# Mask products of the masked experts moved into the first attention, kept as bf16; six buffers for the sorted chunks; shared raw weight buffers

## Chip, cores and metric

The kernel runs on one core of one Trainium2 chip. The metric is the device time of one execution in microseconds. Its engines are TensorE (PE), VectorE (DVE), ScalarE (ACT), GpSimd (POOL) and SyncE (SP, which here issues nearly all transfers). Each works through its own instructions in order and waits for the others by semaphores. SBUF has 128 partitions; PSUM has eight banks of 128x512 f32.

## The reference, cut to what matters

A decoder of two layers over x of 4 x 256 tokens of width 256; after every part comes x = layernorm(x + part(x)). The change touches the first three parts.

```python
# 1: causal attention, 16 heads of 128, weights w_q, w_k, w_v, w_o
x = _layernorm(x + _L0_attn_ref(x, ...))
# 2: a graph: sim = mean over heads of Q K^T of ctx_512
threshold = top_k(sim, 76)[..., -1:]
A = sigmoid(sim) * (sim >= threshold)
A = (A + swapaxes(A)) * 0.5
x = _layernorm(x + (1 - gamma) * x + gamma * A)
# 3: 32 masked experts that share one weight
top1_w, top1_idx = max(softmax(x @ router_w.T))
w_q = clip(round(weight / 0.5), -1, 1)
for e in range(32):
    y = x @ (w_q * scale[:, None] * expert_masks[e]).T
    out = where(top1_idx == e, y * top1_w, out)
x = _layernorm(x + out)
# 4: attention with rotary positions, 5: cross attention, 6: 16 routed experts
```

## The kernel before

The program is a row of blocks: setup, attention layer 0, graph_and_masked_experts, attention layer 1, and the rest. In a block every engine has its own instruction list, and a new block starts on all engines once the old one is finished on all of them.

**First attention.** 16 steps s, each with two heads of two batches; two steps use one group g of weights. In step s PE makes the scores of step s+1, the projections of step s+2, the transposed probabilities and their products with the values; in odd steps also the next group's values and the output projection. POOL splits each raw f32 weight into a high and a low part (split_proj, split_v, split_o, lines 392 and 395), running up to two steps ahead of PE. SP loads the raw weights of group g as soon as the split of the group before has freed their one buffer: q and k after split_proj, v after split_v, o after split_o. Besides, DVE searches each row's 76th largest sim in eight rounds spread over the steps (its copy is L975), and near the end (keep, L993 and L996) sets the entries below it to zero, using the raw q and k buffers for the tanh values. POOL also splits kv and kvt for later use (split_keys) and makes the ternary weight c.tern at s = 9.

**Masked experts.** The 32 masks, each 256x256 f32 (256 KB), are handled in 16 pairs. SP loads a pair into one of four raw buffers (two of their own, c.kv and c.kvt). POOL multiplies pairs 0 to 11 with c.tern (L1345), DVE pairs 12 to 15 (L1518), into four bf16 buffers. PE transposes a pair into one of two PSUM banks (turn, L1381) and ACT copies it to the weight array w (copied, L1458), bank by bank. Meanwhile DVE and POOL do norm 1 (moments L1079 and L1082, roots L1103 to L1110, applied in L1505 together with the graph's entries), norm 2 (applied in L1511), then x is transposed and split (L1143, L1149, L1155), the router's logits are made (L1185, L1186, L1193), DVE finds each row's expert (L1535 to L1543), PE counts ranks (L1388, L1391) and DVE works out each row's place among the sorted rows (L1551 to L1566). POOL scatters the rows to DRAM by eight indirect transfers (L1356). Then come six chunks of 512 sorted rows: a chunk is loaded (L1311) into one of two buffers, turned by PE (L1401), split by ACT and DVE (L1465, L1585), and multiplied with each tile's expert weight (L1417, L1418). ACT evicts to one of two staging buffers (L1474), SP stores them (L1318), and POOL gathers all rows back (L1362). A chunk's buffer is loaded again when the chunk has been turned; SP issues these loads between the stores. keep_warm (L134) issues products on an idle tile.

The last part of SP's list in before:

```python
weights.first_loads(sp)
sp.wait_ge(s_scattered, 16 * NT)
...
sorted_load(0)
sorted_load(1)
for q in range(CHUNKS):
    if q + 2 < CHUNKS:
        sorted_load(q + 2)
    for r in range(2 * q, 2 * q + 2):
        store(r)
```

Of the kernel before, what the change touches and what calls it, by code (L numbers as in the profile page):

```python
# [67 lines left out]
def decoder(nc, a, out):  # L68
    with ExitStack() as ctx:
# [23 lines left out]
        c.ffn_weight, c.clipped, c.tern = sb("ffn_weight", [P, KC, D]), sb("clipped", [P, KC, D]), sb("tern", [P, KC, D], BF16)  # L93
# [242 lines left out]
class AttentionWeights:  # L336
# [12 lines left out]
    def __enter__(self):  # L349
# [4 lines left out]
        self.raw = {n: sb(f"raw_{n}", shape[n]) for n in "qkvo"}  # L354
# [24 lines left out]
    def first_loads(self, sp):  # L379
        for n in "kqvo":  # L380
            self.load(sp, n, 0)
# [36 lines left out]
    def second_splits(self, pool):  # L418
        self.split_all(pool, "v", 0, self.s_split_v)

# [34 lines left out]
def attention(c, layer, weights):  # L455
# [36 lines left out]
    with ExitStack() as ctx:  # L492
# [48 lines left out]
        with nc.Block() as block:  # L541
            @block.sync
            def _(sp):
                for g in range(1, LAST_GROUP + 1):
# [13 lines left out]
            def _(pool):  # L558
# [24 lines left out]
                def ternary():  # L583
# [6 lines left out]
                    nc.gpsimd.tensor_scalar(c.tern[:], c.ffn_weight[:], -12582912.0, None, ALU.add)  # L590

# [5 lines left out]
                def split_keys(part):  # L597
# [15 lines left out]
                    elif part == 3:  # L613
# [3 lines left out]
                        nc.gpsimd.tensor_tensor(c.kvg_lo[:], weighted, f32(c.kvg_hi[:]), ALU.subtract)  # L617
# [11 lines left out]
                for s in range(LAST + 1):  # L629
# [10 lines left out]
                    if not rope and s == 9:  # L640
                        ternary()

# [420 lines left out]
class Norm:  # L1063
# [34 lines left out]
    def root(self, pool, half, eps=EPS, factor=None, squares=None):  # L1098
# [3 lines left out]
        if squares is None:  # L1102
            self.nc.gpsimd.tensor_scalar(self.shifted[:, part], self.mv[:, part, 1], eps, None, ALU.add)  # L1103
# [9 lines left out]
    def roots(self, pool, factor=None):  # L1113
# [52 lines left out]
class Router:  # L1166
# [3 lines left out]
    def __init__(self, c, name, sb, w, experts, raw_banks, out):  # L1170
        self.c, self.nc, self.w, self.experts, self.raw_banks, self.out = c, c.nc, w, experts, raw_banks, out
        self.flat = sb(f"{name}_flat", [2 * experts, NTOK])
# [36 lines left out]
def graph_and_masked_experts(c, weights):  # L1209
# [22 lines left out]
    DVE_PAIRS = range(12, PAIRS)  # L1232
    YBANKS, YSTEPS = 4, -(-TILES0 // 2)
    MAGIC = 12582912.0
    with ExitStack() as ctx:
# [6 lines left out]
        router = Router(c, "b_router", sb, c.rt, EXPERTS0, (c.banks[4], c.banks[6]), c.banks[5])  # L1242
# [725 lines left out]
```

## Time and profile before

| what | value |
|---|---|
| median of 3 runs | 927.09 us (926.79 to 928.6) |
| profiled execution, its own time | 930.73 us |
| its span, first to last instruction | 928.9 us |
| PE busy | 811.1 us (87%) |
| DVE busy | 594.8 us (64%) |
| POOL busy | 492.2 us (53%) |
| ACT busy | 429.9 us (46%) |
| mean granted TensorE clock | 0.943 of full speed |

The profiled execution took 1.8 us more than its span. Busy shares are means over stages with different limits. The first attention runs to about 327.5 us, the masked experts from 327.8 to about 455 us, and the second attention follows.

### The profile page before, as it was taken

The numbers are of one execution on the slowest core, as the hardware profiler recorded it, in microseconds if no ns is written. First come the engines' busy times: TensorE is split into PE (matmuls) and PEld (weight loads), VectorE is DVE, ScalarE is ACT, GpSimd is POOL, SyncE is SP. The second block draws the span as 40 slices with busy tenths as digits, with TensorE's granted clock in tenths as the row PEclk, the third lists the DMA queues.
The fourth block names the chain that finished last, engine by engine and source line by source line (L and its number), as shares of the span: only waits on it lengthen the run. The fifth ranks groups of instructions, "written<-read, shape, count | busy, mean of one in ns | idle before, by whom it ended". The sixth has DMA issues, their size and how long they took to land. (4 is left out here: it accounts for less than half of the span.)

```text
span 928.9 us, 14587 instructions
## 1 busy us (share of the span) xinstructions
PE 811.1 (87%) x4745; PEld 691.0 (74%) x4745; DVE 594.8 (64%) x1655; ACT 429.9 (46%) x1209; POOL 492.2 (53%) x407
## 2 busy tenths in 40 slices
PE   7899999999999836583788999999888499999995
PEld 5678888888888725282477888888776288888885
DVE  4796876866966599311666777767655745455555
ACT  5264644634635515152356665566563532322223
POOL 4757368647440166703255546464521447777774
PEclk8999999999999958897799999999999789999998
DMA  6220620220200057453001110111001001111111
GB/s 194 69 91 1 227 91 1 91 92 1 91 23 1 1 165 238 163 158 91 29 0 53 52 51 3 51 52 52 16 8 36 11 18 51 51 51 34 50 40 46
DMA packets 58331, 59.09 MB, mean 64 GB/s; under 512 B 5392, under 2 KB 49312, under 8 KB 58272
## 3 DMA queue, kind: packets, MB, share of 16 engines
q1 hardware_dynamic: 57504, 56.24, 19.5%
q0 software_dynamic: 768, 2.10, 0.7%
q8 instruction: 32, 0.52, 0.2%
q14 instruction: 27, 0.22, 0.1%
HBM read 50.00 MB, written 8.32 MB: 63 GB/s over the span
## 5 line engine op out<-in xcount | busy, mean ns | idle before, releaser
L829 ACT ACTIVATE a_probs<-bank,a_neg_peak 128x128 f32<-128x128 f32 (+1 forms) x256 | 103.5, 429 | 91.8 <-DVE a_neg_peak L937 91.8
L857 ACT ACTIVATE a_probs<-a_probs,a_row_inv 128x128 f32<-128x128 f32 (+1 forms) x256 | 92.0, 447 | 19.8 <-DVE a_row_inv L945 19.8
L937 DVE CUSTOM_DVE_ANT_0 bank<-bank,causal 128x128 f32<-128x128 f32 (+1 forms) x256 | 82.5, 393 | 20.3 <-PE bank L699 19.2
L835 ACT ACTIVATE a_probs_t<-bank 128x512 f32<-128x512 f32 x96 | 53.9, 597 | 75.7 <-PE bank L719 75.7
L1694 POOL TENSOR_TENSOR d_h_lo<-d_h,d_h_hi 128x512 fp32r<-128x512 f32 x40 | 51.8, 1297 | 52.8 <-ACT d_h_hi L1813 39.3
L738 PE MATMUL bank<-a_probs_t,a_vals 128*128 128x256 f32 x256 | 76.5, 380 | 0.0
L392 POOL TENSOR_TENSOR a_wk_hi<-a_raw_k,one 128x512 fp32r<-128x512 f32 (+1 forms) x24 | 21.7, 902 | 102.4 <-DMA a_raw_k<-in_L_attn_w_k_dram 39.7
L112 PE MATMUL bank<-a_wo_hi,a_ot_hi 128*128 128x256 f32 x256 | 74.4, 291 | 0.7 <-DVE a_ot_lo L957 0.7
L1899 DVE TENSOR_TENSOR d_h<-d_silu,bank 128x512 f32<-128x512 f32 x40 | 27.5, 688 | 73.2 <-PE bank L114 73.1
L113 PE MATMUL bank<-a_wo_lo,a_ot_hi 128*128 128x256 f32 x256 | 73.0, 285 | 0.0
L114 PE MATMUL bank<-a_wo_hi,a_ot_lo 128*128 128x256 f32 x256 | 73.0, 285 | 0.0
L134 PE MATMUL bank<-idle 128*128 128x512 bf16 x110 | 36.6, 505 | 34.1 <-DVE x L1591 15.2
L1906 DVE SCALAR_TENSOR_TENSOR x<-bank,d_gate,x 128x256 f32<-128x256 f32 x160 | 64.6, 476 | 2.6 <-PE bank L114 0.2
L113 PE MATMUL bank<-xt_lo,d_w_hi 128*128 128x512 f32 x160 | 64.0, 400 | 0.0
L112 PE MATMUL bank<-xt_hi,d_w_hi 128*128 128x512 f32 x160 | 63.9, 399 | 0.0
L114 PE MATMUL bank<-xt_hi,d_w_lo 128*128 128x512 f32 x160 | 63.8, 399 | 0.0
L705 PE MATMUL bank<-a_keys,a_queries 128*128 128x256 f32 x256 | 62.3, 388 | 0.0
L719 PE MATMUL bank<-ident,a_probs 128*128 128x128 f32 x384 | 53.4, 275 | 6.1 <-ACT a_probs_t L835 6.1
L719 PEld LDWEIGHTS bank<-ident,a_probs 128*128 128x128 f32 x384 | 44.3, 140 | 16.5 <-ACT a_probs_t L835 10.8
L581 POOL TENSOR_TENSOR a_queries<-sim 128x512 f32<-128x512 f32 x32 | 40.7, 1278 | 29.2 <-DVE sim L912 29.2
L912 DVE TENSOR_TENSOR sim<-bank,a_sin 64x512 f32<-64x512 f32 x80 | 55.1, 688 | 1.1
L829 ACT ACTIVATION_READ_ACCUMULATOR a_probs<-bank,a_neg_peak 128x1 f32 x256 | 55.1, 215 | 0.0
(303 smaller groups left out, 2454.3 us busy)
## 6 DMA issues: line engine op xcount, KB each, us to landing
d_raw<-in_L_ffn_we_dram SPq DMA_DIRECT2D x48, 128.0 KB, 2.2
a_raw_k<-in_L_attn_w_k_dram SPq DMA_DIRECT2D x8, 512.0 KB, 6.3
a_raw_q<-in_L_attn_w_q_dram SPq DMA_DIRECT2D x8, 512.0 KB, 5.3
a_raw_v<-in_L_attn_w_v_dram SPq DMA_DIRECT2D x8, 512.0 KB, 7.2
a_raw_o<-in_L_attn_w_o_dram SPq DMA_DIRECT2D x8, 512.0 KB, 3.7
b_raw<-_L_ffn_expert_masks_dram SPq DMA_DIRECT2D x16, 256.0 KB, 3.2
a_raw_q<-in_L_attn_Wq_dram SPq DMA_DIRECT2D x8, 512.0 KB, 4.9
a_raw_o<-in_L_attn_Wo_dram SPq DMA_DIRECT2D x8, 512.0 KB, 3.6
```

The costliest lines, as they stand in the source:

```text
L112: nc.tensor.matmul(out, l_hi, r_hi, start=start, stop=False)
L113: nc.tensor.matmul(out, l_hi, r_lo, start=False, stop=False)
L114: return nc.tensor.matmul(out, l_lo, r_hi, start=False, stop=stop)
L705: last = nc.tensor.matmul(out, queries[:, j, row + P:row + T], keys[:, j % keys.shape[1], row:row + width], start=True, stop=True)
L719: last = nc.tensor.transpose(c.banks[3 + turned % 2][:, slot % 4 * P:(slot % 4 + 1) * P], probs[s % 2][:, i, at:at + P], c.ident[:])
L738: nc.tensor.matmul(out, vals_of(s)[:, 2 * i, cols], probs_t[:, at:at + T], start=True, stop=False)
L829: nc.scalar.activation(probs[s % 2][:, i, at:at + width], c.banks[i][:, at:at + width], ACT.Exp, bias=neg_peak[:, n:n + 1], scale=-1.0, ac ...
L835: nc.scalar.activation(probs_t[:, i * BANK:(i + 1) * BANK], c.banks[3 + (3 * s + i) % 2][:], ACT.Copy).then_inc(s_pt_free, 1)
L857: last = nc.scalar.activation(part, part, ACT.Copy, scale=row_inv[:, s % 2, n + r:n + r + 1])
L912: last = nc.vector.tensor_tensor(two(across[to:to + HALF_BLOCK, n % 2]), two(bank[at:at + HALF_BLOCK]), many(sin[at:at + HALF_BLOCK], HALF ...
L937: last = nc.vector.tensor_tensor_reduce(part, part, mask, -1.0, 3e38, ALU.add, ALU.min, neg_peak[:, n + r:n + r + 1])
L1906: last = nc.vector.scalar_tensor_tensor(c.x[:, t], c.banks[4 + u][:, (t % 2) * D:(t % 2 + 1) * D], g, c.x[:, t], ALU.mult, ALU.add, accum_ ...
```

## The change

- A new object Masks makes all 16 masked pairs on POOL during the first attention and keeps them all, as bf16: eight pairs in a new tile c.spare, two where the ternary weight was made (c.small), and two each in the raw v, o and q weight buffers. The raw masks pass through c.kv and c.kvt. SP issues their loads within the attention's list, and POOL makes pairs 0, 1 in step 10, 2, 3 in step 12, 4, 5 in step 13, 6 to 11 in step 14 and 12 to 15 in the last step, once DVE has kept its entries.
- The raw weight buffers belong to the program now and are shared by both attentions.
- In the masked experts DVE and POOL make no masks. PE turns eleven pairs before x is transposed, in place of three pairs and twelve warming products, and the others between the router's steps. DVE's small operations on the counters stand ahead of the subtractions of the transposed x.
- The factor of norm 1's root, 2 - gamma, is put into the power's argument as its square's reciprocal, made once in the first attention.
- Six chunk buffers: all six loads are issued one after the other once the scatters have landed, with one semaphore for chunk 0, one for 1 and 2, one for 3 to 5.
- The next attention's raw o weights are loaded behind the last store, and its v weights are split once the last chunk has been turned. Several small tiles move into c.sim.

```diff
+        c.less_sq, c.minus_two = sb("less_sq", [P, 1]), sb("minus_two", [P, 1])
+        c.raw = {n: sb(f"raw_{n}", [DH, GROUP, D] if n == "o" else [P, KC, GROUP * DH]) for n in "qkvo"}
+        c.spare = sb("spare", [P, 4, 2 * BANK])
+        c.masks = Masks(c)
...
+class Masks:
+    PAIRS, RAW = EXPERTS0 // 2, 2
+
+    def __init__(self, c):
+        self.c, self.nc = c, c.nc
+        as_pair = lambda ap: ap.rearrange("p (e k d) -> p e k d", e=2, k=KC)
+        flat = lambda ap: ap.rearrange("p k n -> p (k n)")
+        self.raw = [as_pair(flat(c.kv[:])), as_pair(c.kvt[:])]
+        homes = [flat(home).bitcast(BF16) for home in (c.spare[:], c.small[:], c.raw["v"][:], c.raw["o"][:], c.raw["q"][:])]
+        size = 2 * KC * D
+        self.masked = [as_pair(home[:, at:at + size]) for home in homes for at in range(0, home.shape[-1], size)]
+        self.AFTER_VALUES, self.AFTER_KEPT = 10, 12
...
+    def load(self, sp, pair):
+        if pair == 0:
+            sp.wait_ge(self.s_spare, 1)
+        elif pair >= self.RAW:
+            sp.wait_ge(self.s_masked, pair - self.RAW + 1)
+        for e in range(2):
+            sp.dma_start(self.raw[pair % self.RAW][:, e], self.c.a["L0_ffn_expert_masks"][2 * pair + e].rearrange("(k p) i -> p k i", p=P)).then_inc(self.s_raw[pair % self.RAW], 16)
+
+    def mask(self, pool, pair):
+        pool.wait_ge(self.s_raw[pair % self.RAW], (pair // self.RAW + 1) * 32)
+        wide = self.c.tern[:].unsqueeze(1).broadcast_to([P, 2, KC, D])
+        self.nc.gpsimd.tensor_tensor(self.masked[pair], self.raw[pair % self.RAW], wide, ALU.mult).then_inc(self.s_masked, 1)
...
@@ attention, SP @@
                         sp.wait_ge(s_split_v, g)
                         weights.load(sp, "v", g)
+                    if not rope and g == LAST_GROUP:
+                        for pair in range(4, 6):
+                            c.masks.load(sp, pair)
                     sp.wait_ge(s_split_o, g)
                     weights.load(sp, "o", g)
+                    if not rope and g >= 5:
+                        for pair in ((0, 1), (2, 3), range(6, c.masks.PAIRS))[g - 5]:
+                            c.masks.load(sp, pair)
...
@@ attention, GpSimd @@
+                MASKED_AT = {10: (0, 1), 12: (2, 3), 13: (4, 5), 14: range(6, c.masks.AFTER_KEPT), LAST: range(c.masks.AFTER_KEPT, c.masks.PAIRS)}
+
+                def masks(s):
+                    for pair in MASKED_AT.get(s, ()):
+                        if pair == c.masks.AFTER_KEPT:
+                            pool.wait_ge(s_kept, 1)
+                            pool.drain()
+                        c.masks.mask(pool, pair)
...
@@ Norm.root @@
-            self.nc.gpsimd.tensor_scalar(self.shifted[:, part], self.mv[:, part, 1], eps, None, ALU.add)
+            self.nc.gpsimd.tensor_scalar(self.shifted[:, part], self.mv[:, part, 1], eps, factor, ALU.add, ALU.mult)
...
-        if factor is not None:
-            pool.drain()
-            last = self.nc.gpsimd.tensor_scalar(self.rstd[:, part], self.rstd[:, part], factor[:], None, ALU.mult)
...
@@ masked experts, SP @@
-                for pair in range(RAW):
-                    load(pair)
                 sp.dma_start(numbers[:], a["numbers"]).then_inc(s_numbers, 16)
-                for pair in range(RAW, PAIRS):
-                    load(pair)
-                weights.first_loads(sp)
+                sp.wait_ge(s_turned, PAIRS)
+                weights.first_loads(sp, "kqv")
                 sp.wait_ge(s_scattered, 16 * NT)
-                sp.wait_ge(s_masked, DVE_PAIRS.start)
-                sp.wait_ge(s_masked_dve, len(DVE_PAIRS))
-                sorted_load(0)
-                sorted_load(1)
                 for q in range(CHUNKS):
-                    if q + 2 < CHUNKS:
-                        sorted_load(q + 2)
+                    sp.dma_start(sorted_x[q], c.sorted_rows[slots_of(q)].rearrange("(t p) d -> p t d", p=P)).then_inc(s_sorted[load_of[q]], 16)
+                for q in range(CHUNKS):
                     for r in range(2 * q, 2 * q + 2):
                         store(r)
+                sp.wait_ge(s_stored[1], 16 * CHUNKS)
+                weights.load(sp, "o", 0)
...
@@ masked experts, GpSimd @@
-                norm1.roots(pool, c.one_less)
-                for pair in range(0, 2):
-                    mask(pair)
+                norm1.roots(pool, c.less_sq[:])
                 norm2.roots(pool)
-                for pair in range(2, DVE_PAIRS.start):
-                    mask(pair)
...
+                pool.wait_ge(s_turned, PAIRS)
                 weights.first_splits(pool)
+                pool.wait_ge(s_xt, XT + CHUNKS * KC)
                 weights.second_splits(pool)
...
@@ masked experts, TensorE; ScalarE's copies go in the same order @@
-                    pe.wait_ge(s_sorted[q % 2], 16 * (q // 2 + 1))
+                    pe.wait_ge(s_sorted[load_of[q]], 16 * len(LOADED[load_of[q]]))
...
-                for pair in range(0, 3):
+                for pair in range(0, 11):
                     turn(pair)
-                norm1.wait(pe, 1)
-                keep_warm(c, 12)
                 turned2.pe(pe, s_norm2, 4)
-                for pair in range(3, 5):
+                for pair in range(11, 13):
                     turn(pair)
                 router.raw_pe(pe, turned2)
-                for pair in range(5, 7):
-                    turn(pair)
+                turn(13)
                 router.logits_pe(pe)
-                for pair in range(7, 9):
+                for pair in range(14, PAIRS):
                     turn(pair)
                 rank()
-                for pair in range(9, PAIRS):
-                    turn(pair)
...
@@ masked experts, VectorE @@
-                turned2.dve(dve)
...
                 nc.vector.tensor_scalar(numbers[:], numbers[:], -float(EXPERTS0), None, ALU.add)
+                turned2.dve(dve)
...
-                for pair in DVE_PAIRS:
-                    mask(pair)
```

## Rows read from the trace of the kernel before

**Rows 1.** The page, its first line.

```profile
span 928.9 us, 14587 instructions
```

**Rows 2.** Windows: length; busy PE, PEld, DVE, ACT, POOL (count); PE clock, DMA share, GB/s.

```profile
94.00:130.00 36.00, 36.00 (x212) 31.67 (x211) 26.98 (x87) 18.18 (x58) 20.80 (x14) 1.00 0.42 143
...
328.00:374.00 46.00, 23.16 (x191) 17.41 (x192) 42.72 (x80) 18.79 (x23) 32.23 (x22) 0.70 0.71 223
```

**Rows 3.** Timeline of DVE, 331 to 374 us: start, duration, engine, line, operation.

```profile
331.72 1.67 DVE L1505 SCALAR_TENSOR_TENSOR x<-x,b_b_norm_rstd,sim 128x256 f32<-128x256 f32 x4 [0.28 <-POOL b_b_norm_rstd L1110]
...
335.24 3.76 DVE L1505 SCALAR_TENSOR_TENSOR x<-x,b_b_norm_rstd,sim 128x256 f32<-128x256 f32 x4
...
340.86 10.90 DVE L1511 SCALAR_TENSOR_TENSOR x<-x,b_b_norm_mv,b_b_norm_rstd 128x256 f32<-128x256 f32 x8
...
353.13 1.29 DVE L1155 TENSOR_TENSOR xt_lo<-bank,xt_hi 128x512 fp32r<-128x512 f32 x2 [0.18 <-ACT xt_hi L1149]
...
360.19 0.41 DVE L1535 TENSOR_REDUCE b_top<-bank 128x8 f32<-128x256 f32 x1
...
361.20 1.33 DVE L1539 SCALAR_TENSOR_TENSOR b_found<-b_above,b_numbers 128x256 f32<-128x256 f32 x1
...
363.10 1.69 DVE L1543 TENSOR_TENSOR b_chosen<-b_found,b_first 128x256 bf16<-128x256 f32 x1
...
369.47 1.22 DVE L1518 TENSOR_TENSOR ffn_weight<-kvt,tern 128x1024 bf16<-128x1024 f32 x1
370.61 0.18 DVE L1551 TENSOR_SCALAR b_segments<-bank 128x32 f32<-128x32 f32 x1
...
373.45 0.17 DVE L1566 CAST b_place<-b_place_f 128x8 uint32<-128x8 f32 x1
```

**Rows 4.** Timeline of POOL, its first masks.

```profile
333.55 4.38 POOL L1345 TENSOR_TENSOR b_masked<-b_raw,tern 128x1024 bf16<-128x1024 f32 x2
```

**Rows 5.** Timeline of PE and ACT, 356 to 374 us.

```profile
356.54 1.97 PE L1193 MATMUL bank<-pick,b_b_router_flat 64*128 64x32 f32 x16
...
365.06 1.17 PE L1391 MATMUL bank<-b_chosen,b_every 128*128 128x256 bf16 x8
...
369.34 4.69 ACT L1458 ACTIVATE b_w<-bank 128x1024 fp32r<-128x1024 bf16 x5 [0.28 <-PE bank L1381]
```

**Rows 6.** The chunks: PE's timeline, PE's waits (total, times, longest), the loads' landing.

```profile
391.97 1.09 PE L1401 MATMUL bank<-ident,kvt 128*128 128x128 f32 x8 [0.25 <-DMA kvt<-sorted_rows]
...
PE bank L1401 <- DMA kvt<-sorted_rows: 3.4, 3, 2.0
...
DMA to landing us min/median/max: 3.8/4.5/5.3
```

**Rows 7.** POOL and DVE by time; SP's issue of a mask pair; L975 in all; mask loads' landing.

```profile
108.74 1.04 POOL L392 TENSOR_TENSOR a_wk_hi<-a_raw_k,one 128x512 fp32r<-128x512 f32 x1 [16.93 <-PE bank L114]
...
127.76 0.98 DVE L975 COPY a_work<-sim 128x256 f32<-128x256 f32 x1
...
242.25 1.04 POOL L392 TENSOR_TENSOR a_wk_hi<-a_raw_k,one 128x512 fp32r<-128x512 f32 x1 [7.52 <-DMA a_raw_k<-in_L_attn_w_k_dram]
...
301.74 1.89 POOL L392 TENSOR_TENSOR a_wo_hi<-a_raw_o,one 128x1024 fp32r<-128x1024 f32 x1 [31.32 <-PE bank L114]
...
314.92 1.67 DVE L996 SCALAR_TENSOR_TENSOR sim<-sim,thr,a_raw_k 128x256 f32<-128x256 f32 x4
...
326.24 1.28 DVE L964 TENSOR_TENSOR x<-x,bank 128x512 f32<-128x512 f32 x2
...
344.70 0.88 SPq L1305 DMA_DIRECT2D kv<-_L_ffn_expert_masks_dram  x2
...
L975 DVE COPY a_work<-sim x8: 281/283/4250, 35.3 to 270.7; 128x256 f32<-128x256 f32 x8
...
DMA to landing us min/median/max: 2.8/3.3/5.5
```

More of the change, by code:

```diff
@@ L92, in decoder @@
         c.rows = sb("rows", [P, 5, D])
-        c.ffn_weight, c.clipped, c.tern = sb("ffn_weight", [P, KC, D]), sb("clipped", [P, KC, D]), sb("tern", [P, KC, D], BF16)
+        c.small = sb("small", [P, 2, KC * D])
+        c.ffn_weight, c.clipped = (c.small[:, i].rearrange("p (k d) -> p k d", k=KC) for i in range(2))
+        c.tern = sb("tern", [P, KC, D], BF16)
         c.s_ffn_weight, c.s_rows = c.sem("ffn_weight"), c.sem("rows")
@@ L377, in load, with first_loads @@
         sp.dma_start(self.raw[n][:], part).then_inc(self.s_raw[n], 16)
-    def first_loads(self, sp):
-        for n in "kqvo":
+    def first_loads(self, sp, which="kqvo"):
+        for n in which:
             self.load(sp, n, 0)
@@ L616, in split_keys @@
                         pool.drain()
-                        nc.gpsimd.tensor_tensor(c.kvg_lo[:], weighted, f32(c.kvg_hi[:]), ALU.subtract)
+                        nc.gpsimd.tensor_tensor(c.kvg_lo[:], weighted, f32(c.kvg_hi[:]), ALU.subtract).then_inc(c.masks.s_spare, 1)
                 if rope:
@@ L641, in _ @@
                         ternary()
+                    if not rope:
+                        masks(s)
             @block.tensor
@@ L1096, in squares, with root @@
             last.then_inc(self.s_var, 1)
-    def root(self, pool, half, eps=EPS, factor=None, squares=None):
+    def root(self, pool, half, eps=EPS, factor=1.0, squares=None):
         part = slice(HALF_TILES[half].start, HALF_TILES[half].stop)
@@ L1241, in graph_and_masked_experts @@
         turned3 = Transposed(c, "b_turned", turned2, XT + CHUNKS * KC)
-        router = Router(c, "b_router", sb, c.rt, EXPERTS0, (c.banks[4], c.banks[6]), c.banks[5])
-        top, above, likely = sb("top", [P, NT]), sb("above", [P, NT, EXPERTS0]), sb("likely", [P, NT, EXPERTS0])
+        router = Router(c, "b_router", sb, c.rt, EXPERTS0, (c.banks[4], c.banks[6]), c.banks[5], flat=c.sim[0:2 * EXPERTS0, 0:NTOK // T].rearrange("p t n -> p (t n)"))
+        top = sb("top", [P, NT])
+        above, likely, found = (c.sim[:, NT // 2 + i].rearrange("p (t e) -> p t e", t=NT) for i in range(3))
         total, weight = sb("total", [P, NT]), sb("weight", [P, NT])
-        numbers, found, first = sb("numbers", [P, NT, EXPERTS0]), sb("found", [P, NT, EXPERTS0]), sb("first", [P, NT])
+        numbers, first = sb("numbers", [P, NT, EXPERTS0]), sb("first", [P, NT])
         chosen = sb("chosen", [P, NT + 1, EXPERTS0], BF16)
@@ L1297, in _ @@
             def _(sp):
-                def load(pair):
-                    if pair >= RAW:
-                        if pair - RAW in DVE_PAIRS:
-                            sp.wait_ge(s_masked_dve, pair - RAW - DVE_PAIRS.start + 1)
-                        else:
-                            sp.wait_ge(s_masked, pair - RAW + 1)
-                    for e in range(2):
-                        sp.dma_start(raw[pair % RAW][:, e], a["L0_ffn_expert_masks"][2 * pair + e].rearrange("(k p) i -> p k i", p=P)).then_inc(s_raw[pair % RAW], 16)
-                def sorted_load(q):
-                    if q >= 2:
-                        sp.wait_ge(s_xt, XT + KC * (q - 1))
-                    sp.dma_start(sorted_x[q % 2], c.sorted_rows[slots_of(q)].rearrange("(t p) d -> p t d", p=P)).then_inc(s_sorted[q % 2], 16)
                 def store(r):
@@ L1485, in _ @@
                 nc.scalar.activation(likely[:], above[:], ACT.Exp).then_inc(s_likely, 1)
-                for pair in range(9, PAIRS):
-                    copied(pair)
                 high(0)
```

60 lines of the change are left out of this document (24 added, 36 removed).

## The prediction

> **What bounds the kernel now.** I read the page first for the span [rows 1], then busy time by stage [rows 2], then the timelines of VectorE (DVE), GpSimd (POOL), TensorE (PE) and ScalarE (ACT) in the stages that the change touches. In a stretch of the first attention PE is busy for the whole of it: 36.00 of 36.00 us [rows 2]. PE sets the time there, and whatever DVE or POOL does is free until it makes PE wait. In the stretch from 328 to 374 us it is the other way round: PE is busy 23.16 of 46 us at a granted clock of 0.70, DVE 42.72 us [rows 2]. Here the chain runs through DVE: two normalizations, the router, the choice of expert, the place of each row.
>
> DVE is busy there but mostly not at work. The same operation on the same 128x256 tile takes 0.42 us each in one group of four and 0.94 us each in the next, and the eight that follow take 1.36 us each [rows 3]. The slow ones lie under POOL's mask products, 2.2 us each [rows 4]. Subtractions that read PSUM, further on, keep their 0.64 us [rows 3]. So operations whose inputs are all in SBUF wait for POOL's current instruction. Four masks made by DVE itself, 1.22 us each, then stand between the choice of expert and the places: DVE chose at 364.79 (363.10 + 1.69) and reads the ranks only at 370.61 [rows 3].
>
> **The stage with the normalizations.** I follow DVE with all masks gone from DVE and POOL.
> 1. The scale factor of the first norm goes into the power's argument, and the POOL operation L1110 falls away. DVE idled 0.28 us for it before L1505 [rows 3]: gain 0.3.
> 2. The second group of L1505 takes 1.67 instead of 3.76 us [rows 3]: gain 2.1.
> 3. L1511 runs eight times in 10.90 us; at 0.42 each it is 3.3 [rows 3]: gain 7.6. POOL's second-norm root comes about 1.6 us after its moments, while the other half's tile work takes 1.7, so it stays just hidden. Were it not, up to 1 us is lost. Sum 10.0.
> 4. Seven small DVE operations (the counters) now precede the four subtractions. Uncovered by POOL I take 1.2 us for them, from 0.28 for a 128x256 copy [rows 7] and 0.17 or 0.18 for the small ones [rows 3]; bounds 0.6 and the 5.8 us that they span now (354.4 to 360.2 [rows 3]). On the path: loss 1.2.
> 5. The last subtraction ends at 354.42 and the router's logits at 358.51 (356.54 + 1.97 [rows 5]), 4.1 us later, but DVE reads them at 360.19 since the small operations are still under way [rows 3]. With those moved ahead, the 4.1 us remain of 5.8: gain 1.7.
> 6. L1539 and L1543 take 1.33 and 1.69 us; at 0.42 each that is a gain of 2.2 [rows 3].
> 7. After the choice only the rank products remain: they end at 366.23 (365.06 + 1.17 [rows 5]). DVE starts at 370.61, and could at 366.3: gain 4.3.
>
> The places, ready at 373.62 [rows 3], so come 10.0 - 1.2 + 1.7 + 2.2 + 4.3 = 17.0 us earlier. The scatters and all behind them hang on the places and move with them.
>
> **What has to hide there.** Sixteen pairs still pass through PE and ACT. ACT copies five in 4.69 us, 0.94 each [rows 5]; eleven from 328.9 on (the block's start and one turn of about 1 us) end at 339.3, and the first normalized half is ready at 340.2 by my steps. Only 0.9 us of cover: if PE stays at the low clock, each of its turns is as long as a copy, and 1 us may show. The twelve warming products are gone as well; the bound for a low clock in transposes and router is 0 to 2 us. The pace of 0.94 us already had PE at high clock, so I take 0. The other five pairs lie between steps whose DVE work is longer.
>
> **The sorted chunks.** In before PE waited 3.4 us in three waits for the transfer of a chunk, 0.25 of it ahead of the second [rows 6]. With six buffers these go. But chunks 1 and 2 now share a semaphore: the second turn waits for the third transfer. Landing ran from 3.8 to 5.3 us, the second of two queued behind the first [rows 6], so a third queued is some 1.5 us later still. Net gain 3.4 - 0.25 - 1.5 = 1.6; bounds -1.5 (nothing won, since the stores' two buffers become the limit) and 3.1. The value weights' split waits for the last chunk's turn now and ends, 4.3 us of POOL work later, well ahead of the last store; the output weights' load goes behind the stores, where the next attention needs it only after its first two head pairs.
>
> **The first attention.** POOL takes sixteen masks instead of twelve: 35 us in all. It has the room: it idled 31.32 us before 301.74 alone [rows 7].
> - SP's queue: after each output weight load come mask loads, 1 MB before the next q, k and v. POOL's split behind them begins at 242.25 now, 7.5 us waited for its transfer [rows 7]. Two masks (4.4 us) push the output split and so the loads; four mask loads add 2 us of issue (0.88 for two [rows 7]) and up to 3 of transfer. I get 251 instead of 242.25. The same position four weight groups earlier was as late in before: its split began at 108.74 after a wait of 16.93 [rows 7], where the one at 242.25 had waited 7.5. PE had 36.00 of 36.00 in that stretch [rows 2]. So this lateness costs nothing. SP also stands at the load of pair 4 until mask 2 is done; behind it is only the output load, due at 301.74.
> - Pairs 6 to 11 alternate between two raw buffers: a load takes 0.9 to issue and 3.3 to land [rows 7], a mask 2.2 [rows 4], so two pairs need 6.5 us. From 280 on they end near 299, ahead of the last output split at 301.74 [rows 7].
> - DVE's copy L975 takes 0.28 us as a rule, took 0.98 under POOL at 127.76, within the full stretch, and once 4.25 [rows 7]. Two more may meet POOL work, up to 2.2 us each: I take 0.3, bounds 0 and 4.4.
>
> The Trainium skill, "SBUF — State Buffer", section "Who interferes with whom", says that a DVE copy in a two-port mode, or a DVE operation with both inputs in SBUF against a POOL operation that reads SBUF, is blocked for the other's whole instruction. By that rule alone, with both blocked copies charged to PE, the sum would be 4.4 us worse; the trace agrees with the blocking (0.98 for 0.28) and not with the charge.
>
> - The tail: pairs 12 to 15 wait until DVE has kept its entries, at 316.59 (314.92 + 1.67 [rows 7]). Masks 12 and 13 end at 321.1; load 14 is issued at 319.0 and lands at 323.2, load 15 at 321.1 and 325.4; mask 15 ends at 327.6. DVE's last addition ends at 327.52 [rows 7], and the next block starts for all engines together behind it. I charge 0.3. With landings of 5.5 us, the maximum [rows 7], it is 2.5; nothing is below 0.
>
> The skill, "GPSIMD Engine Reference", section 4.1, advises against GpSimd for a two-input elementwise operation, at about twice DVE's time. The trace agrees (2.2 against 1.22 us). Were the four pairs moved from DVE all exposed in the tail, it would take 4 us from the gain.
>
> **Sum.** 17.0 + 1.6 - 0.3 - 0.3 = 18.0 us. The profiled execution took 930.73 us around a span of 928.9 [rows 1], so 912.7; it is 3.6 above the median of the runs, 927.09, from which I subtract the same: 909.1 us.
>
> **Rivals.**
> - A, as above: 906.5 to 913, chance 0.62.
> - B, the stall is gone but PE and ACT hold the stage: low clock, the eleven copies as a gate (2 to 3 us), stores limiting the chunks (3), tail late (2.5). For it speaks the clock of 0.70 [rows 2]. 913 to 919, chance 0.25.
> - C, more gain than summed (small operations 0.6, chunks 3.1, second norm's wait none): 904 to 906.5, chance 0.07.
> - D, slower: the raw buffers' pace. If pairs 6 to 11 needed over 7 us each instead of 3.3, mask 11 would end past 313; the output split queues behind it on POOL, DVE's ten keeping operations wait 1 to 1.8 us each for the masks, and the last four masks end 18 us late, at 345.5, where all gain is spent. At 9 us each it would be about 935. Against it: landings of 3.3 and at most 5.5 us with an otherwise idle queue. Chance 0.03.
> - E, PE waits for a late projection split and gives back most: 919 to 927, 0.03, against which the 108.74 row stands.
>
> Measurement can tell 0.2%, 1.9 us, from no change. Faster: A, B, C and most of E, 0.95; same 0.02; slower 0.03. The range takes A with part of B and C: 905.5 to 916.5.
>
> **What would show it.** Right: L1505 and L1511 near 0.42 us each; places some 29 us after the block's first moments, which begin at 327.8, instead of 45.8; no wait of PE for a chunk after the second; the first attention's stretch still full. Wrong: PE idle for a POOL split between 200 and 300; a mask on POOL after DVE's last addition; PE at low clock from the first turn to the router; evictions waiting for stores in every chunk.

## The result and the profile after

The changed kernel takes 902.47 us (median of 4 runs, 900.31 to 906.13), the kernel before 926.94 on the same chip: a ratio of 0.974 with a 95% interval of 0.970 to 0.978. The gain is 24.5 us, against 18.0 forecast, and the time lies 3 us below the range's lower end. A second comparison in five rounds gave 901.38 us and 0.9743 (0.9717 to 0.9768). Times of different groups of runs below come from different chips, on which the kernel before had medians of 926.5 (both kernels again, late weights, idle delay), 926.54 (masks put back, chunk loads) and 924.37 us (everything with warming products); across groups the ratios to the kernel before are the fair comparison.

The span of the changed kernel's profile is 901.7 us, with 14551 instructions. Its windows over the same full stretch of the first attention as before and over the block with the normalizations (compare [rows 2]; columns as there):

```profile
94.00:130.00 36.00, 36.00 (x213) 31.62 (x212) 27.05 (x87) 18.17 (x58) 20.57 (x14) 1.00 0.42 144
329.00:358.00 29.00, 17.75 (x178) 14.64 (x179) 21.56 (x77) 18.69 (x23) 5.84 (x8) 0.85 0.18 52
```

POOL's 32.23 busy us of the block have become 5.84. What that does to DVE is in its timeline (L1505 of before is L1521 now, L1511 is L1527, L1155 is L1212, and so on in order; compare [rows 3]):

```profile
329.55 1.41 DVE L1139 BATCH_NORM_STATS2 b_b_norm_stats<-x 128x6 f32<-128x256 f32 x4 [0.32 <-PEq L580]
...
336.56 1.64 DVE L1521 SCALAR_TENSOR_TENSOR x<-x,b_b_norm_rstd,sim 128x256 f32<-128x256 f32 x4
...
340.05 3.42 DVE L1527 SCALAR_TENSOR_TENSOR x<-x,b_b_norm_mv,b_b_norm_rstd 128x256 f32<-128x256 f32 x8
...
344.03 0.29 DVE L1539 TENSOR_SCALAR b_numbers<-b_numbers 128x256 f32<-128x256 f32 x1
344.42 2.48 DVE L1212 TENSOR_TENSOR xt_lo<-bank,xt_hi 128x512 fp32r<-128x512 f32 x4
350.91 0.42 DVE L1544 TENSOR_REDUCE b_top<-bank 128x8 f32<-128x256 f32 x1 [4.01 <-PE bank L1250]
...
352.93 0.42 DVE L1552 TENSOR_TENSOR b_chosen<-sim,b_first 128x256 bf16<-128x256 f32 x1
354.82 0.19 DVE L1557 TENSOR_SCALAR b_segments<-bank 128x32 f32<-128x32 f32 x1 [1.47 <-PE bank L1414]
...
357.67 0.17 DVE L1572 CAST b_place<-b_place_f 128x8 uint32<-128x8 f32 x1
```

The places are ready 28.3 us after the block's first moments instead of 45.8. The chunks of sorted rows, in PE's timeline and its one wait (compare [rows 6]):

```profile
375.17 1.69 PE L1424 MATMUL bank<-ident,kvt 128*128 128x128 f32 x8
377.76 1.09 PE L1424 MATMUL bank<-ident,kv 128*128 128x128 f32 x8 [0.90 <-DMA spare<-sorted_rows]
382.89 1.03 PE L1424 MATMUL bank<-ident,spare 128*128 128x128 f32 x8
387.42 1.03 PE L1424 MATMUL bank<-ident,spare 128*128 128x128 f32 x8
391.95 1.03 PE L1424 MATMUL bank<-ident,spare 128*128 128x128 f32 x8
396.47 1.03 PE L1424 MATMUL bank<-ident,spare 128*128 128x128 f32 x8
```

In before the turns behind the one shown in [rows 6] stood as follows (with the first product of a chunk behind two of them):

```profile
398.06 1.04 PE L1401 MATMUL bank<-ident,kv 128*128 128x128 f32 x8
398.86 0.36 PE L1417 MATMUL bank<-b_w,xt_hi 128*64 x1
...
404.91 1.09 PE L1401 MATMUL bank<-ident,kvt 128*128 128x128 f32 x8 [2.02 <-DMA kvt<-sorted_rows]
406.33 0.33 PE L1417 MATMUL bank<-b_w,xt_hi 128*64 x1 [0.33 <-issue]
...
410.18 1.03 PE L1401 MATMUL bank<-ident,kv 128*128 128x128 f32 x8
...
416.11 1.09 PE L1401 MATMUL bank<-ident,kvt 128*128 128x128 f32 x8 [1.10 <-DMA kvt<-sorted_rows]
```

And the first attention of the changed kernel (POOL's late projection split, an early mask, the output split and the last mask; DVE's copy L975, now L1035, and its last addition L964, now L1024; compare [rows 7]):

```profile
250.03 1.04 POOL L398 TENSOR_TENSOR a_wk_hi<-raw_k,one 128x512 fp32r<-128x512 f32 x1 [11.34 <-DMA raw_k<-in_L_attn_w_k_dram]
265.15 2.13 POOL L458 TENSOR_TENSOR spare<-kv,tern 128x1024 bf16<-128x1024 f32 x1
302.20 1.89 POOL L398 TENSOR_TENSOR a_wo_hi<-raw_o,one 128x1024 fp32r<-128x1024 f32 x1 [5.87 <-PE bank L120]
325.02 2.14 POOL L458 TENSOR_TENSOR raw_q<-kvt,tern 128x1024 bf16<-128x1024 f32 x1
```

```profile
235.06 1.30 DVE L1035 COPY a_work<-sim 128x256 f32<-128x256 f32 x1
327.95 1.28 DVE L1024 TENSOR_TENSOR x<-x,bank 128x512 f32<-128x512 f32 x2
```

From each profile I take the start times that separate the stages: the block's first moments, the places' cast, the first load of a chunk, the first gather of expert outputs, the first load of the second attention's weights, and the load that opens the last block. Lengths in us (from places to first chunk load it is 13.2 in all):

| profile | block starts | moments to places | chunks | gather to 2nd attention | 2nd attention | rest |
|---|---|---|---|---|---|---|
| before, first profile | 327.84 | 45.61 | 42.48 | 26.59 | 250.93 | 222.21 |
| before, second | 325.34 | 45.62 | 42.63 | 26.57 | 245.57 | 221.95 |
| after, first | 329.55 | 28.12 | 39.37 | 25.58 | 244.40 | 221.45 |
| after, second | 326.44 | 28.87 | 38.02 | 25.34 | 246.18 | 221.54 |
| mean of before less mean of after | -1.4 | 17.1 | 3.9 | 1.1 | 3.0 | 0.6 |

The differences add to 24.3 us. 17.1 and 3.9 belong to stages that I had summed at 17.0 and 1.6. The 3.0 of the second attention was in no sum; its products and their order are the same in both kernels (its raw weight buffers and first loads are not).

### The profile page after: what moved, and what is told of

Its sections match the earlier page's. It is cut to its first block and busy times, and to the rows that moved or that the text cites. A ratio compares the mean times of both kernels' runs of the same rounds, so it can differ in the third digit from the quotient of the medians.

```text
span 901.7 us, 14551 instructions
## 1 busy us (share of the span) xinstructions
PE 801.8 (89%) x4733; PEld 685.0 (76%) x4733; DVE 574.4 (64%) x1651; ACT 429.2 (48%) x1209; POOL 499.8 (55%) x411
## 5 line engine op out<-in xcount | busy, mean ns | idle before, releaser
L398 POOL TENSOR_TENSOR a_wk_hi<-raw_k,one 128x512 fp32r<-128x512 f32 (+1 forms) x24 | 21.6, 901 | 102.3 <-DMA raw_k<-in_L_attn_w_k_dram 64.1
L140 PE MATMUL bank<-idle 128*128 128x512 bf16 x98 | 32.7, 505 | 35.3 <-DVE x L1597 16.3
```

## The experiments

There are two theories for the second attention, where the first pair of profiles differed by 6.5 us: a **clock theory** (PE's granted clock and its waits vary from one execution to the next), and a **structure theory** (shared raw buffers, later loads and splits make this attention shorter). For the stages that did change, each term is put back by itself.

**Both kernels again.** No edit, five rounds.

> The kernel before, unchanged. The two profiled runs differ by 27.2 us, the medians by 24.5, and 6.5 us of the 27.2 lie in the second attention, where before shows TensorE's granted clock below full speed in six stretches of 5 us and the changed kernel in none. Clock theory: the low stretches are not a property of this code; another execution of the same kernel has them elsewhere or not at all, the second attention takes between 244.4 and 251 us with fewer or other low stretches, and the times of this kernel spread by 3 us or more. Structure theory: the second attention takes 250.9 us again within 1 us, with low stretches at the same offsets from its start.

> The changed kernel, unchanged. Clock theory: the second attention takes between 244.4 and 251 us, and another execution can have low stretches. Structure theory: 244.4 us again within 1 us. Both: the ratio to the kernel before near 0.974; five rounds narrow its interval.

Measured: before 924.44 us (920.46 to 930.91, 12 runs), its second attention 245.57 us; after 901.38 (899.03 to 903.85, 6 runs), its second attention 246.18. The structure theory asked for 250.9 and 244.4 again and is out. In the first profile of before, PE had waited 2.23 us for POOL deep in this attention, and the clock was low behind the wait (PE's timeline, then windows with the granted clock in the third column from the right):

```profile
653.02 1.97 PE L699 MATMUL bank<-a_keys,a_queries 128*128 128x128 f32 x8 [2.23 <-POOL a_queries L581]
```

```profile
652.00:654.00 2.00, 0.98 (x5) 0.98 (x6) 0.00 (x0) 0.00 (x0) 1.97 (x2) 0.79 0.00 0
654.00:656.00 2.00, 2.00 (x8) 1.80 (x8) 0.97 (x8) 0.00 (x0) 1.27 (x1) 0.50 0.00 0
656.00:658.00 2.00, 2.00 (x9) 1.64 (x8) 1.40 (x9) 1.83 (x9) 0.00 (x0) 0.85 0.00 0
```

The second profile of before has one of 0.91 us there. Waits of 0.9 to 2.2 us for the rotated queries stand at 49 to 51, 77, 105 to 109 or 194 to 198 us of the second attention in some profiles of both kernels and in others not. Over the 14 profiles of this study the second attention took 244.2 to 250.9 us, and 250.7 in one that has all of the change.

**The late half of the shared buffers, in the kernel before.**

```diff
-                weights.first_loads(sp)
+                weights.first_loads(sp, "kqv")
...
+                sp.wait_ge(s_stored[1], 16 * CHUNKS)
+                weights.load(sp, "o", 0)
...
                 weights.first_splits(pool)
+                pool.wait_ge(s_xt, XT + CHUNKS * KC)
                 weights.second_splits(pool)
```

> Only the late half of the shared buffers, put into the kernel before: the next attention's raw output weights are loaded after the last store of expert outputs, and its value weights are split after the last chunk is turned. Structure theory (the second attention gains because its weights are loaded and split later): the second attention shortens from 250.9 to about 244.4 us and the time falls by about 6.5 us, to about 920.5. Clock theory: the second attention keeps what its clock gives it and nothing here lies on the path, so the time stays within 2 us of the kernel before (the split leaves the chunk stage and could give at most 1.5 us there).

Measured: 926.70 us against 926.5, ratio 1.0005 (0.9981 to 1.0028); second attention 246.08 us, chunks 44.24. The late loads and the late split give nothing in the attention, and nothing in all. The chunk stage of this one profile is 1.6 to 1.8 us longer than in before: the step behind the wait of 2.22 us for a chunk took 6.84 us instead of 5.27 and 5.01, at a granted clock of 0.50 in its middle (408 to 410 us). The stretch from gather to second attention is 1.2 shorter.

**A stage of 18.2 us put between attention and block.**

```diff
+        with nc.Block() as block:
+            @block.vector
+            def _(dve):
+                for _ in range(8):
+                    nc.vector.memset(scratch[:, 0:8], 0.0)
+                    dve.drain()
```

> The changed kernel with 8 fillings of a matrix by VectorE in a stage of their own between the first attention and the normalizations, nothing else; each is 128x2048 elements, so the stage is estimated at 9 to 18 us. Everything behind it is shifted and the code there is untouched. Structure theory: everything behind the stage keeps its length, the second attention 244.4 us within 1 us, and the time rises by the stage's own length. Clock theory: shifted in time, the second attention can catch low stretches; it takes up to 251 us, and the time rises by the stage's length plus up to 6.5 us, or minus 1 to 2 us if the shift takes low stretches away elsewhere.

Measured: 922.34 us (10 runs), 21.0 above 901.38. The stage runs from 328.48 to 346.69, 18.2 us, the second attention takes 245.63. From DVE's last addition to the block's first moments it is 19.0 us (327.70 to 346.69) instead of 0.3, so the delay itself is 18.7 and some 2.3 us come on top by the medians, 1.1 by the ratios. In the profile the first attention had already ended 1.6 us later than in the second of after (327.70 for 326.12), ahead of anything that the delay can touch, and the stretch from gather to second attention is 1.4 longer. Then the same with PE multiplying zeros in that stage:

```diff
+            @block.tensor
+            def _(pe):
+                keep_warm(c, 84)
```

> The stage of 18.2 us between first attention and normalizations again (8 fillings by VectorE), but TensorE multiplies zeros in it throughout (84 products). With TensorE idle in that stage the time rose by 20.8 us, 2.5 beyond the stage. Idle theory: the excess is what an idle TensorE costs behind the stage (granted clock at its lower level when work comes back, 0.78 in the first 9 us of the block against 1.00 without the stage); here it goes, and the time is 901.4 + 18.2 = 919.6 within 1 us. Shift theory: only the shift in time changes where low stretches fall, and the excess of about 2.5 us stays: 922.

Measured: 920.95 us (12 runs), ratio 0.9963 (0.9940 to 0.9986), against 0.9957 (0.9935 to 0.9979) for the idle form: no difference, where 2.5 us was asked for. But the stage was not 18.2 us here. PE's 84 products ran for 19.98 us, from 325.64 to 345.62, so PE and not DVE ended it, and from the last addition to the first moments it is 21.3 us (324.58 to 345.92), 2.3 more than in the idle form. With 21.0 us for the delay the time lies 1.4 us below kernel plus delay by the medians and 0.6 below by the ratios. The intervals leave about 3 us either way for each form, so this settles neither theory: a delay costs about its own length, and whether an idle PE adds to it stays open.

**POOL's twelve products back in the block.** The first term, by itself.

```diff
                 norm1.roots(pool, c.less_sq[:])
+                pool.wait_ge(s_turned, 1)
+                for pair in range(0, 2):
+                    mask(pair)     # drain, then again <- raw mask x c.tern, used by nobody
                 norm2.roots(pool)
+                for pair in range(2, 12):
+                    mask(pair)
+                pool.drain()
```

> The changed kernel, and GpSimd multiplies 12 pairs once more in the block (2 behind the first norm's roots, 10 behind the second's), as before the change; their products are written over a matrix already turned and used by nobody. Contention theory (steps 2, 3 and 6 of the prediction): the eight L1527 go from 0.43 to about 1.36 us, four of the L1521 from 0.42 to about 0.94, and the three elementwise operations of 0.4 us behind the logits slow down: 7.6 + 2.1 + 2.2 = 11.9 us; the small VectorE operations now lie ahead of the router's subtractions and would add their slowed part, 4.8 us at most. Time 913 to 918. Rival (the block gained because turns and copies were moved ahead, not from GpSimd's silence): less than 4 us, 905 or below.

Measured: 916.38 us (8 runs), ratio to before 0.9909 (0.9873 to 0.9945), so 15.0 above the changed kernel, and 15.1 above the kernel with fine semaphores (below), which ran on the same chip; moments to places 42.67 us instead of 28.12 and 28.87. DVE's timeline of this kernel (L1533 is L1521 of after, L1539 its L1527, L1546 to L1551 the small operations, L1564 the choice), then POOL's:

```profile
334.54 4.55 DVE L1533 SCALAR_TENSOR_TENSOR x<-x,b_b_norm_rstd,sim 128x256 f32<-128x256 f32 x4
...
340.94 9.03 DVE L1539 SCALAR_TENSOR_TENSOR x<-x,b_b_norm_mv,b_b_norm_rstd 128x256 f32<-128x256 f32 x8
...
350.11 1.90 DVE L1546 TENSOR_SCALAR b_earlier<-causal 128x128 bf16<-128x128 bf16 x1
...
352.25 2.13 DVE L1551 TENSOR_SCALAR b_numbers<-b_numbers 128x256 f32<-128x256 f32 x1
...
364.17 1.70 DVE L1564 TENSOR_TENSOR b_chosen<-sim,b_first 128x256 bf16<-128x256 f32 x1
```

```profile
345.30 2.12 POOL L1379 TENSOR_TENSOR spare<-kvt,tern 128x1024 bf16<-128x1024 f32 x1
```

Against after: 2.9 in the group of four, 5.6 in the group of eight, 3.5 in the small operations (0.19 and 0.29 us each without POOL's work), 1.3 in the choice: 13.3 of the 13.8 to 14.6 us by which the stage grew. Besides POOL's waits and drains for these products nothing else in the kernel differs; turns and copies keep their new places. The rival of under 4 us is out.

The Trainium skill, "SBUF — State Buffer", section "Who interferes with whom", names these forms: two SBUF inputs, or a copy-like operation in a two-port mode. The trace agrees on both, 1.13 us for 0.43 and 2.13 for 0.29, and the four L1212 in between, which read PSUM, take 2.47 us as against 2.48. The prediction's own wording, that operations whose inputs are all in SBUF wait, is too wide. In before a reduction with one SBUF input stands between the slow L1539 and L1543 while POOL multiplies, and takes its usual time:

```profile
362.61 0.42 DVE L1541 TENSOR_REDUCE b_first<-b_found 128x8 f32<-128x256 f32 x1
```

**DVE's four products back.**

```diff
                 ... wide(first), ALU.is_equal).then_inc(s_chosen, 1)
...
+                for pair in range(4):
+                    dve.drain()
+                    nc.vector.tensor_tensor(again, c.masks.raw[pair % 2], c.tern[:]..., ALU.mult)
```

> The changed kernel, and VectorE multiplies 4 pairs once more between the choice of expert and the ranks, as before the change (products used by nobody). Step 7 of the prediction: 4 of about 1.2 us, less the 1.4 us that VectorE now waits for the ranks there, so 3.5 us more, time about 905. Rival: the ranks and what follows are late for another reason, and under 1 us shows.

Measured: 908.10 us (5 runs, ratio 0.9816, 0.9772 to 0.9859), moments to places 32.33 us, 3.5 above the second profile of after and 4.2 above the first. DVE's timeline shows the wait of 1.47 gone and the last product before the ranks:

```profile
354.20 1.23 DVE L1559 TENSOR_TENSOR spare<-kvt,tern 128x1024 bf16<-128x1024 f32 x1
355.35 0.18 DVE L1564 TENSOR_SCALAR b_segments<-bank 128x32 f32<-128x32 f32 x1
```

In its own stage the term is as expected. The time rose by 6.7, 3.2 more; half the interval of the ratio is 4 us, and in the profile the chunks took 40.04 us and the second attention 247.65, 2.0 and 1.5 more than in the second of after, within what both vary by. These products did not wait for anything; in before one of the four waited for a bank to be turned, which no experiment put back:

```profile
367.19 1.23 DVE L1518 TENSOR_TENSOR b_masked<-b_raw,tern 128x1024 bf16<-128x1024 f32 x1 [1.26 <-PE bank L1381]
```

**The chunk loads as before, two ahead**, and a kernel to compare it with, in which only the semaphores are one for each chunk:

```diff
-        LOADED = (range(0, 1), range(1, 3), range(3, CHUNKS))
+        (fine: one semaphore for each chunk)
...
+                def sorted_load(q):                       (two ahead)
+                    if q >= 2:
+                        sp.wait_ge(s_xt, XT + KC * (q - 1))
...
+                sorted_load(0)
+                sorted_load(1)
                 for q in range(CHUNKS):
+                    if q + 2 < CHUNKS:
+                        sorted_load(q + 2)
...
-                    pe.wait_ge(s_sorted[load_of[q]], 16 * len(LOADED[load_of[q]]))
+                    pe.wait_ge(s_sorted[q][0], s_sorted[q][1] + 16)     (both)
```

> The changed kernel with the chunk loads issued as before: two at first, each further one when the chunk two before it is turned, and queued in with the stores; a semaphore for each chunk. Theory (the loads' order is the whole chunk gain): the stretch from the first load to the first gather goes from 38.0-39.4 back to 42.5, and the time rises by 3 to 4.5 us, to 904.5-906. The prediction's size: 1.6 us, 903. Rival (the stretch gained from the value weights' split moved behind it, or from clock): under 1 us.

> The changed kernel with a semaphore for each chunk, nothing else: chunk 1 no longer waits for chunk 2's load, nor chunk 3 for those of 4 and 5. If the wait of 0.9 to 1.9 us before chunk 1 is turned lies on the path, it gives 0.5 to 1 us, 900.5; if the stores' pace sets the evictions behind it, nothing. It is also what the kernel with the loads two ahead is to be compared with.

Measured: two ahead 905.67 us (5 runs, ratio 0.9787, 0.9749 to 0.9825), chunks 44.42 us; fine 901.25 (5 runs, ratio 0.9729, 0.9685 to 0.9774), chunks 38.45. PE's timeline, the turns of chunks 2 to 5 of two ahead, and a window behind the second of them; then the first product of chunk 0 in fine, and in the second profile of after:

```profile
378.80 1.03 PE L1428 MATMUL bank<-ident,spare 128*128 128x128 f32 x8
386.38 1.97 PE L1428 MATMUL bank<-ident,spare 128*128 128x128 f32 x8 [2.89 <-DMA spare<-sorted_rows]
392.40 1.03 PE L1428 MATMUL bank<-ident,spare 128*128 128x128 f32 x8
398.29 1.10 PE L1428 MATMUL bank<-ident,spare 128*128 128x128 f32 x8 [1.20 <-DMA spare<-sorted_rows]
```

```profile
387.00:391.00 4.00, 4.00 (x27) 4.00 (x26) 1.38 (x2) 2.00 (x4) 0.00 (x0) 0.69 0.38 129
```

```profile
376.13 0.33 PE L1438 MATMUL bank<-b_w,xt_hi 128*64 x1 [1.51 <-DVE xt_lo L1589]
```

```profile
376.38 0.33 PE L1440 MATMUL bank<-b_w,xt_hi 128*64 x1
```

The order of the loads alone gives 6.0 us of stretch and 4.4 of time, so it covers the whole of the stage's gain of 3.9. It is more than that in this profile because the waits are dearer: behind the one of 2.89 us the granted clock was 0.69 (the window above), and the step took 6.02 us, where the two profiles of before kept a clock of 1.00 there and needed 5.27 and 5.01. In the ten profiles with all loads issued at once the stage took 38.0 to 40.5 us. The shared semaphore costs nothing that shows. Without it chunk 1 is turned 5.8 us after the first load (373.58 less 367.83) instead of 6.9 (375.43 less 368.52), but PE then stands 1.51 us for the low part of chunk 0, and the first product comes 8.3 us after the first load, against 7.9 with the semaphore shared and 7.6 in the second profile of before.

**Warming products**, in three kernels: 11 in the block, where PE is idle behind the eleventh turn; 14 ahead of the last output projection of both attentions, where PE waits 3.4 us; and both.

```diff
                 for pair in range(0, 11):
                     turn(pair)
+                keep_warm(c, 11)
                 turned2.pe(pe, s_norm2, 4)
...
                     pe.wait_ge(s_split_o, LAST_GROUP + 1)
+                    if 0 in heads:
+                        pe.wait_ge(s_pt_free, 3 * PAIRS_OF_HEADS - 3)
+                        keep_warm(c, 14)
```

> The changed kernel with 11 warming products put back between the eleventh turn and the transposes of the normalized rows, where TensorE stands idle for 2.45 us. The kernel before had 12 in front of these transposes and the change took them out, which the prediction bounded at 0 to 2 us and took at 0. In the profile of the changed kernel the 16 transposes behind the idle time take 3.75 us at the low clock and the router's first products 0.72. Theory (the removed products cost something): places 1.5 to 2 us earlier, time 899.5. Rival (the chain runs through VectorE's L1527 and ScalarE, which don't depend on the clock): under 0.5 us.

> The changed kernel with 14 warming products in the 3.41 us for which TensorE waits ahead of the last output projection, in both attentions. In six of ten profiles so far the granted clock falls to its lower level 1 to 4 us behind this wait and stays there for 3 to 4 us, in the first attention nearly always. Clock theory: these stretches go and each gives about 1.5 us: 2 to 3 us in all, time 898.5 to 899.5, and the spread of the runs narrows. Rival (TensorE isn't what ends the attentions; ScalarE's copies are): under 0.5 us. Third way: the products push the last projection back by up to 0.2 us in each attention and cost 0.4.

> Both kinds of warming products in the changed kernel; candidate to be faster than both kernels. If both theories hold the gains add: 3.5 to 5 us, 896.5 to 898. If the clock's low stretches only move elsewhere, under 1 us.

Measured, 6 runs each: block 905.28 us, where 899.5 was asked for, ratio 0.9788 (0.9749 to 0.9827); tail 898.74, 0.9724 (0.9687 to 0.9761); both 899.52, 0.9732 (0.9697 to 0.9767). The products in the tail do to the clock what was expected: it was 1.00 in all of both tails in both kernels that have them. In the second profile of after, at the end of the first attention (windows as above):

```profile
310.00:312.00 2.00, 1.15 (x5) 1.09 (x6) 2.00 (x4) 2.00 (x7) 0.00 (x0) 0.56 0.00 0
312.00:314.00 2.00, 2.00 (x12) 1.94 (x11) 1.93 (x6) 0.58 (x2) 0.00 (x0) 0.58 0.04 8
```

and with the products in the tail:

```profile
310.00:312.00 2.00, 2.00 (x17) 1.93 (x16) 1.93 (x5) 1.52 (x4) 0.00 (x0) 1.00 0.04 8
312.00:314.00 2.00, 2.00 (x19) 1.88 (x17) 2.00 (x6) 0.28 (x1) 0.00 (x0) 1.00 0.00 0
```

In the block the 16 transposes of the normalized rows took 3.75 us in the second profile of after and 1.95 with warming products:

```profile
338.64 3.75 PE L1200 MATMUL bank<-ident,x 128*128 128x128 f32 x16 [2.45 <-DVE x L1527]
```

```profile
337.42 1.95 PE L1200 MATMUL bank<-ident,x 128*128 128x128 f32 x16
```

There the places came 27.19 us after the moments, 1 to 1.7 earlier than in the two profiles of after; but the kernels with fine semaphores and with products in the tail alone had 27.17 and 27.19 without anything added in the block. So the block's gain can't be told from what varies by itself, and as a whole that kernel was 3.9 us slower than the changed one by the medians. Its profile has the long form of the second attention (250.69 us); the kernel with both kinds has the same products in the block and took 899.52, so the loss is not theirs for certain either. The tail's products are 2.6 us below the changed kernel by the medians, but the kernel before was 2.1 faster on that chip as well. By the ratios, 0.9724 for 0.9743, it is 1.8 us, and their intervals, 0.9687 to 0.9761 and 0.9717 to 0.9768, overlap: a version that is clearly faster than the kernel before, and not shown to be faster than the changed one.

## Why the prediction was wrong in size, point by point

- **The block, 17.0 forecast, 17.1 measured** (17.5 in the first pair). Steps 1 to 3: no wait for the root is left, the second L1521 group takes 1.64 us (1.67 forecast), the eight L1527 3.42 (3.3). Step 4: the small operations span 1.0 us (343.42 to 344.42; 1.2 forecast). The eleven copies ended at 340.38, and PE waited 2.4 us for the normalized rows behind its turns, so they stayed hidden. Step 5: from the last subtraction (346.90) to the read of the logits it is 4.0 us (4.1 forecast). Step 6: 0.42 each, as said. Step 7: DVE reads the ranks 1.47 us after the choice ends, as forecast (366.3 less 364.79); 3.5 to 4.2 of the 4.3 us came back with the four products. That POOL's silence carries the bulk is shown: its twelve products alone bring back 13.8 to 14.6 us.
- **The chunks: 1.6 forecast, 3.1 in the first pair of profiles, 3.9 as the mean of two pairs, 6.0 in the experiment. The step that failed, and the largest part of the miss.** As the prediction put it: "Net gain 3.4 - 0.25 - 1.5 = 1.6; bounds -1.5 ... and 3.1." The 1.5 charged for the shared semaphore is 0 to 0.3, since the product behind the turn waits for chunk 0's low part if the turn comes early. And the waits in the records are not all that a late chunk costs. From turn to turn the changed kernel takes 4.53 us (382.89 to 387.42 and so on). In before the last three steps, from 398.06 to 416.11, are 6.85, 5.27 and 5.93, which is 2.3, 0.7 and 1.4 too long, 4.4 in all, where the recorded waits are 2.0 and 1.1. The upper bound of 3.1 took the waits for the whole of it. About half of the other 1.3 can be read: behind the late turn the first product comes 1.42 us after the turn's start (406.33 less 404.91), behind a turn in time 0.80 (398.86 less 398.06), and the profile names nothing that PE waits for in these 0.6 us. The rest is spread over the three steps and was not taken apart. Two other profiles show a further price that before's two did not pay, a low clock behind the same wait, of about 1.5 us.
- **The first attention, 0.3 lost in its length and 0.3 in its tail.** In the pair of profiles the block starts 1.7 us later, in the second pair 1.1. One copy was blocked, 1.30 us for 0.28, and the rows of the first pair place 0.5 of the 1.7 there; the rest goes with a low clock 10 to 18 us ahead of the block's start, behind a wait of 3.4 us that before has too with a shorter stretch behind it. The projection split came at 250.03 for 251 forecast and cost nothing. The last mask ended at 327.16, before DVE's last addition: its 0.3 was 0. Without a delay the changed kernels in the experiments start the block at 324.3 to 327.5, the three profiles of before at 325.3 to 328.3, so no lasting loss is seen.
- **What no sum held.** 1.1 us from gather to second attention, 0.6 behind it, and 3.0 in the second attention, in the two pairs of profiles. Taken over all 14 profiles, each stage from the kernels that leave it unchanged, the means of before less those of the changed kernels are: 0.5 up to the block's start, 17.8 from moments to places, 3.9 in the chunks, 0.3 from gather to second attention, 0.7 in the second attention, 0.6 behind it. That is 23.8 us in all, close to the 23.8 that the ratio of 0.9743 stands for. So most of the 3.0 was luck of the four profiles, and of the 5.8 by which this sum exceeds 18.0, 2.3 are the chunks, 1.6 the three stages that the sum put at nothing, 1.1 the first attention (0.5 for -0.6) and 0.8 the block. The terms below 1 us are smaller than what their stages vary by from profile to profile and have no cause that was shown; before has only three profiles in this, one of them with late weights. One thing speaks against a lasting clock effect in the attentions: the mean granted clock was 0.9485 over 29 runs of before and 0.9553 over 6 of after, which is 47.7 and 40.3 us of lost full clock (0.0515 x 926 and 0.0447 x 901), a difference of 7.4; the block alone accounts for 13.8 less 4.4 us of it (0.30 x 46 [rows 2] and 0.15 x 29). That is argued, not shown.
- **The range.** Rival C, with 3.1 for the chunks, was the one that came nearest, and its bounds still ended at 904. The range's lower end was the lower bound of a sum in which the chunk term had the wrong ceiling, and which had no width for what the unchanged stages vary by.

## What to carry to other kernels

A wait inside a software pipeline is priced by the distance from one turn to the next, with and without it, not by the length that the wait has in the records; and a later arrival is charged only if the next consumer isn't waiting for something else.

Work on an engine that is off the path can still be dear if it slows another engine that is on it: 12 products of 2.1 us on POOL, which was never the bound, were worth 14 us of DVE's time.

Before an unpredicted difference in an untouched stage is explained, look at a second profile of each kernel.

## What the runs showed of the hardware

- The second attention took 244.2 to 250.9 us from one execution to another, 244.3 to 250.7 in the changed kernels that leave its code alone, with waits of 0.9 to 2.2 us of PE for POOL that come and go and low clock behind some of them. Over 29 runs the kernel before spread from 920.16 to 931.19 us, and the longer ones are those with the lower mean clock (correlation -0.77).
- A wait of PE of 3.4 us ahead of the last projection was followed by a granted clock near 0.50 in 18 of the 24 tails without warming products, and in some (the second attention of the first profile of after) not. With 14 products on zeros in the wait the clock was 1.00 in all four tails.
- While POOL ran two-input products of 2.13 us, DVE's two-input operations on 128x256 f32 took 1.13 us instead of 0.43 and a one-input addition of a constant 2.13 instead of 0.29; its one-input reduction kept 0.42 and its subtractions that read PSUM 0.62.
